# The order of VectorE's steps in the first attention phase of a four-layer kernel, and an early exponential on ScalarE

## The chip, the cores and the metric

The kernel runs on one core of a Trainium2 chip. The metric is the device time of one execution in microseconds (us). The median of three runs of the kernel before is 1622.35 us (1619.3 to 1623.19). The engines are TensorE (PE), VectorE (DVE), ScalarE (ACT), GpSimd (POOL) and SyncE (SP, which only issues transfers). Each has its own instruction stream; they meet at semaphores.

## The reference, cut to what matters

Sixteen tiles of 128 tokens with 256 values each go through four layers, each an attention and a feed-forward part. The change lies where layer 0's attention and layer 1's attention are computed:

```
x = x + L0_xattn(layernorm(x), ctx)   # softmax(q k^T + alibi, masked) v, 16 heads of 16, then out_w
x = x + L0_ffn(layernorm(x))          # shared expert, and eight routed experts (top 2)
x = x + L1_xattn(layernorm(x), ctx)   # per token: 16 heads against 16 heads, causal over heads
x = x + L1_ffn(layernorm(x))          # top 2 of eight experts
# layers 2 and 3 follow
```

Layer 0's attention is an ordinary one over 128 keys. Layer 1's is unusual: for each token alone, its 16 query heads attend to the 16 key heads of the same token's context row, so a tile's scores are 16x16 for each token. These are elementwise products and sums and run on DVE.

## The kernel before, in words

**Turns.** The sixteen tiles are four groups of four tiles (T = 4). A turn of `phase1` does layer 0 for one group: context columns, keys, values, query columns, attention, output projection, the residual add, and the shared expert. From the second turn on, the same turn does layer 1's attention for the group before, with its router's lists. So the first turn has none of that other layer's work, and turns 2, 3 and 4 have it. On PE and ACT turns 2 to 4 are one rolled loop; on DVE turns 2 and 3 are a loop, and turn 4 is written out. After turn 4 come the early expert tiles of layer 1, then the other layers.

**Layer 0's attention.** It goes by units: UNITS = 8 in a turn, two for each tile, eight heads in each. For unit n, PE writes a bias and the scores into two PSUM banks ("s"), DVE takes the negated row maxima (`maxima(n)`, line 1841, two reductions of 128x512), ACT takes exponentials (line 1464, eight of 128x128) and with them empties the banks, PE transposes the probabilities ("p", two banks, line 937), ACT copies them (line 1470), and PE multiplies them with the values ("v"). After both units of a tile ACT copies the sum (line 1457), PE transposes it back ("o", line 930), and DVE divides by the row sums (`norm_out(t)`: a reciprocal at line 1848, then a multiplication at line 1779 into `att_rows`). PE's order is `att_order`: at step n it does scores n, probabilities n-2, values n-3, and at odd n from 5 on the result of tile (n-5)/2.

**Banks.** Scores rotate over four banks, so scores n+2 want those of unit n emptied and so on. Probabilities and results rotate together over two banks, 4 and 5 (`PROB_RING`): p of units 0 to 3 take 4 and 5 in turn, tile 0's result takes 4, unit 4's first block takes 5 and its second block takes 4 again, after DVE has divided tile 0. In the same way unit 6's second block follows tile 1's result.

**Pieces.** The other layer's work on DVE is a list of pieces (`layer1_pieces`, `layer1_rows_out`): two for the normalization and the queries; for each of four tiles eight for the scores (four products m0 to m3 of growing width and four sums r0 to r3, in the order m0 m1 r0 m2 r1 m3 r2 r3); scale, largest and shift, with the mark "shifted"; total and inverse; eight for each of four tiles with the values; divide and add; and two for the next normalization, with the mark "end". That makes 75. `some(n)` does the next n of them, `until(mark)` does all up to the mark. Between "shifted" and total stands an exponential on ACT (`exps16`, line 1534). ACT does it in its own order at step `L1_SHIFT` of its loop, behind that unit's exponentials and copies.

**DVE's order in a turn, before.** 10 pieces; then for each unit n its maxima and 4 pieces; behind unit 5 the rest up to "shifted" (three more); behind unit 6's pieces the division of tile 0; then 4 pieces and the division of tile 1, 4 and tile 2, 4 and tile 3; then the remaining 18 pieces. Then it adds the projected rows ("xo") to the residual stream (after GpSimd's `x_biased`) and normalizes them for the feed-forward part.

**Tables.** ACT's exponential and its SiLU (in the feed-forward part) want different activation tables; copies and identities go with either. The loads are put into the program ahead of the activation that wants them.

Of the kernel before, what the change touches and what calls it, by code (L numbers as in the profile page):

```python
# [28 lines left out]
P = 128  # L29
TILES = 16  # L30
T = 4
# [116 lines left out]

L1_FRONT, L1_STEP, L1_SHIFT = 10, 4, 5


LATE = range(1, T)
# [9 lines left out]
def build(nc, ins, out):  # L164
# [7 lines left out]
    UNITS = 2 * T  # L172
# [119 lines left out]
    with ctx:  # L292
        def sb(name, shape, dt=F32):
            return ctx.enter_context(nc.sbuf_tensor(name, shape, dt))
# [55 lines left out]
        NA = sb("norm_rows_layer1", [P, T, D])  # L350
        PRDA = sb("products_dve", [P, 4 * H * HD])
        PAR = sb("head_parity", [P, 2])
        CKM = sb("k_bias_by_parity", [P, KC, 2])
        LGA = sb("router0_logits", [P, TILES * E])
        cT = sb("ctx_cols", [P, KC, T * P])
# [1070 lines left out]
        def _(act):  # L1426
# [6 lines left out]
            def copy_cols(plan, g, name, dst, bias=None):  # L1433

                for m in range(KC):
                    ps, b = full(plan, g, (name, m))
                    if bias is None:
                        act.activation(dst[:, m, :], ps[:, :], ACT.Copy).then_inc(bank_empty[b], 1)
                    else:
                        act.activation(dst[:, m, :], ps[:, :], ACT.Identity, bias=col_bias[:, bias, m:m + 1]).then_inc(bank_empty[b], 1)  # L1440

            def phase1(plan, turn, g, prev):
# [8 lines left out]
                    act.activation(V0[:, t, :, 0:HD], ps[:, 0:D].rearrange("p (h d) -> p h d", h=H), ACT.Copy).then_inc(bank_empty[b], 1)  # L1451
                copy_cols(plan, turn, "xT0", xT)
                copy_cols(plan, turn, "qT", qT, CQ0)
                for n in range(UNITS + 4):
                    if n >= 5 and n % 2 == 1:
                        ps, b = full(plan, turn, ("acc", "oT", (n - 5) // 2))
                        act.activation(OT[:, :], ps[:, :], ACT.Copy).then_inc(bank_empty[b], 1)
                    if n < UNITS:
                        u = n % SB
                        act.wait_ge(sem("maxima"), UNITS * g + (n + 1))  # L1460
                        for x in range(2):
                            ps, b = full(plan, turn, ("s", n, x))
                            for h in range(4 * x, 4 * x + 4):
                                last = act.activation(SC[:, u, h, :], ps[:, (h % 4) * P:(h % 4 + 1) * P], ACT.Exp, bias=MX[:, 32 + 8 * u + h:33 + 8 * u + h])  # L1464
                            last.then_inc(bank_empty[b], 1)
                    if 2 <= n < UNITS + 2:
                        i = n - 2
                        for x in range(2):
                            ps, b = full(plan, turn, ("p", i, x))
                            act.activation(PT[:, i % KB, 4 * x:4 * x + 4, :], ps[:, :].rearrange("p (h k) -> p h k", h=4), ACT.Copy).then_inc(bank_empty[b], 1)  # L1470
                    if n == L1_SHIFT and prev is not None:
                        exps16(prev + 1)
# [270 lines left out]
        def _(dve):  # L1743
# [87 lines left out]
            def phase1(plan, turn, g, prev, last_turn=False):  # L1831
# [4 lines left out]
                def maxima(i):  # L1836

                    for x in range(2):
                        ps, b = full(plan, turn, ("s", i, x))
                        at = 32 + 8 * (i % SB) + 4 * x  # L1840
                        last = dve.tensor_reduce(MX[:, at:at + 4], ps[:, :].rearrange("p (h k) -> p h k", h=4), AX, ALU.max, negate=True)  # L1841
                    last.then_inc(sem("maxima"), 1)

                def norm_out(t):
                    ps, b = full(plan, turn, ("o", t))
                    o = ps[:, :].rearrange("p (h d) -> p h d", h=H)
                    r = RC[:, H * (t % 2):H * (t % 2) + H]
                    d(dve.reciprocal(r, o[:, :, HD]))
                    settle()
                    tt(AO[:, t, :].rearrange("p (h d) -> p h d", h=H), o[:, :, 0:HD], bc(r, HD), ALU.mult).then_inc(bank_empty[b], 1)  # L1850

                some(L1_FRONT)
                for n in range(UNITS):
                    maxima(n)
                    some(L1_STEP)
                    if n == L1_SHIFT:
                        until("shifted")
                    if n >= 6 and n % 2 == 0:
                        norm_out((n - 6) // 2)
                some(L1_STEP)  # L1860
                norm_out(T - 3)
                some(L1_STEP)
                norm_out(T - 2)
                some(L1_STEP)
                norm_out(T - 1)
                until("end")
                dve.wait_ge(sem("x_biased"), g + 1)
                for t in range(T):
# [249 lines left out]
            class Pieces:  # L2118
# [4 lines left out]
                def some(self, count):  # L2123
                    for _ in range(count):
                        while self.left and isinstance(self.left[0], str):
                            self.left.pop(0)
                        if self.left:
                            self.left.pop(0)()

                def until(self, mark):  # L2130
                    while mark in self.left:
                        p = self.left.pop(0)
                        if not isinstance(p, str):
                            p()
# [976 lines left out]
```

## Time and profile before

| what | us |
|---|---|
| median of three runs | 1622.35 |
| the profiled execution's own time | 1619.95 |
| its span in the trace | 1618.2 |
| PE busy | 1325.2 (82%) |
| DVE busy | 830.0 (51%) |
| ACT busy | 448.3 (28%) |
| POOL busy | 286.4 (18%) |
| first maxima of turns 1 to 4 start at | 39.34, 129.74, 251.67, 376.72 |

Times in the rows are counted from the start of the span. An engine's shares are means over stages with different limits: the four turns of the first phase fill the first 460 us or so, and the layers after them the rest. An arrow in square brackets names what ended the idle time in front of an instruction, and how long the idle time was. PE's granted clock is 1.00 at the high and 0.50 at the low level.

### The profile page before, as it was taken

To read this page: it belongs to the slowest core of one execution; us is meant where nothing else is said; L and a number is where in the kernel's file an instruction comes from. 1 tells how busy PE (TensorE), PEld (TensorE's weight loads), DVE (VectorE), ACT (ScalarE), POOL (GpSimd) and SP (SyncE) were. 2 spreads that over 40 slices of the span, in tenths; PEclk is the share of its full clock that TensorE was granted. 3 is DMA by queue.
4 is the path that set the end of the run, shared out by engine and by line. 5 is a ranking of instruction groups with operands and counts; after the bars stand their busy time and mean duration, and the time that the engine had idled before them with its cause. 6 is when DMAs were issued, how large, how long until landed. Compare 5 with 4: busy or idle time off the path is not lost.

```text
span 1618.2 us, 25691 instructions
## 1 busy us (share of the span) xinstructions
PE 1325.2 (82%) x8174; PEld 1081.9 (67%) x8186; DVE 830.0 (51%) x2347; ACT 448.3 (28%) x1126; POOL 286.4 (18%) x307
## 2 busy tenths in 40 slices
PE   5877687677658897889977877868489999999997
PEld 3554454444447677888855656556379999999996
DVE  2249768768776767112244757575752222222222
ACT  2635225325322233111223332323121111111111
POOL 2010012012020002000124334441421111111111
PEclk9787677668668999999977988989799999999999
DMA  9996032023066277888501001010368888888984
GB/s 341 351 264 146 0 99 106 0 86 118 0 226 219 92 275 247 292 290 291 184 22 40 14 27 53 27 40 1 123 249 315 311 311 324 312 310 313 326 315 147
DMA packets 116318, 291.52 MB, mean 180 GB/s; under 512 B 8192, under 2 KB 90528, under 8 KB 101024
## 3 DMA queue, kind: packets, MB, share of 16 engines
q1 hardware_dynamic: 106032, 273.00, 48.4%
q0 software_dynamic: 10224, 17.77, 4.3%
q8 instruction: 30, 0.49, 0.1%
q14 instruction: 32, 0.26, 0.0%
HBM read 218.84 MB, written 71.90 MB: 180 GB/s over the span
## 4 chain that ended last, share of the span: by engine, by line
PE 51%; issue 19%; DVE 13%; POOL 6%; DMA 6%; ACT 3%; SPq 2%; DVEq 0%; POOLq 0%; ACTq 0%
PE bank L838 47%; DMA work<-in_moe 4%; POOL expert_rows_in L2898 3%; DVE work L2518 2%; DVE stats L1785 1%; ACT work L1464 1%; DVE row_max L1841 1%; PE bank L1140 1%; PE bank L937 1%; DVE x_stream L2518 1%; PE bank L1181 1%; DVE extra L2026 1%; POOL rstd L2863 1%; PE bank L845 1%; DVE extra L2029 1%
## 5 line engine op out<-in xcount | busy, mean ns | idle before, releaser
L838 PE MATMUL bank<-norm_cols,work 128*128 128x128 f32 x3488 | 435.2, 280 | 28.7 <-DMA work<-in_moe 17.2
L838 PEld LDWEIGHTS bank<-norm_cols,work 128*128 128x128 f32 x3488 | 424.8, 196 | 43.0 <-issue 24.9
L1779 DVE TENSOR_TENSOR extra<-bank,span 128x256 f32<-128x256 f32 x202 | 85.6, 425 | 386.9 <-ACT span L1563 386.9
L838 PE MATMUL bank<-work,extra 128*128 128x256 f32 x808 | 207.7, 381 | 0.0
L1563 ACT ACTIVATE span<-bank 128x256 f32<-128x256 f32 x202 | 77.4, 383 | 447.9 <-PE bank L838 447.9
L838 PEld LDWEIGHTS bank<-work,extra 128*128 128x128 f32 x808 | 139.0, 192 | 10.9
L3044 POOL DMA_INDIRECT out_x<-att_rows,slot_token x39 | 60.7, 1556 | 345.7 <-ACT att_rows L1573 304.8
L2863 POOL TENSOR_TENSOR rstd<-var_eps,neg_half 128x4 f32<-128x4 f32 x18 | 18.3, 1018 | 515.5 <-DVE var_eps L1791 515.5
L838 PE MATMUL bank<-norm_cols,weights 128*128 128x128 f32 (+2 forms) x416 | 90.8, 378 | 18.2 <-ACT norm_cols L1604 12.0
L838 PE MATMUL bank<-weights,norm_cols 128*128 128x512 f32 (+1 forms) x192 | 88.4, 609 | 8.3 <-ACT norm_cols L1604 5.5
L838 PEld LDWEIGHTS bank<-norm_cols,weights 128*128 128x128 f32 x416 | 68.0, 219 | 35.3 <-ACT norm_cols L1604 16.9
L838 PE MATMUL bank<-work 128*128 128x256 f32 (+4 forms) x260 | 63.9, 386 | 27.6 <-ACT work L1604 12.3
L1464 ACT ACTIVATE work<-bank,row_max 128x128 f32<-128x128 f32 x256 | 69.5, 389 | 44.5 <-DVE row_max L1841 44.4
L937 PE MATMUL bank<-ident,work 128*128 128x128 f32 x256 | 55.4, 378 | 29.3 <-DVE att_rows L1779 23.0
L1841 DVE TENSOR_REDUCE row_max<-bank 128x4 f32<-128x512 f32 x64 | 41.1, 684 | 66.9 <-PE bank L838 66.9
L937 PEld LDWEIGHTS bank<-ident,work 128*128 128x128 f32 x256 | 41.1, 192 | 47.1 <-DVE att_rows L1779 25.5
L838 PEld LDWEIGHTS bank<-work 128*128 128x128 f32 (+1 forms) x260 | 40.9, 203 | 45.0 <-ACT work L1604 11.7
L838 PEld LDWEIGHTS bank<-weights,norm_cols 128*128 128x128 f32 x192 | 40.3, 223 | 41.7 <-issue 27.8
L2870 POOL TENSOR_TENSOR rstd<-var_eps,neg_half 128x2 f32<-128x2 f32 x48 | 35.4, 738 | 174.0 <-DVE var_eps L1791 173.6
L838 PE MATMUL bank<-weights,ctx_cols 128*128 128x256 f32 x192 | 49.9, 416 | 0.0
L838 PE MATMUL bank<-work,q_cols 32*128 32x256 f32 x256 | 49.5, 518 | 0.0
L838 PEld LDWEIGHTS bank<-weights,ctx_cols 128*128 128x128 f32 x192 | 40.2, 214 | 7.9 <-issue 2.2
(361 smaller groups left out, 1978.6 us busy)
## 6 DMA issues: line engine op xcount, KB each, us to landing
work<-in_moe SPq DMA_DIRECT2D x39, 2048.0 KB, 8.1
work<-in_moe SPq DMA_DIRECT2D x70, 1024.0 KB, 9.4
expert_rows_in<-zero SPq DMA_DIRECT2D x3, 5590.0 KB, 52.3
expert_rows_in<-zero SPq DMA_DIRECT2D x3, 5504.0 KB, 36.0
expert_rows_out<-zero SPq DMA_DIRECT2D x3, 5504.0 KB, 22.4
work<-in_moe SPq DMA_DIRECT2D x31, 512.0 KB, 5.9
weights<-in_moe SPq DMA_DIRECT2D x8, 1024.0 KB, 5.6
att_cols<-expert_rows_in SPq DMA_DIRECT2D x39, 130.0 KB
```

The costliest lines, as they stand in the source:

```text
L838: return pe.matmul(o, l, r, start=a, stop=z)
L845: m = pe.transpose(ps[:, t * P:(t + 1) * P], rows[:, t, c * P:(c + 1) * P], ident[:, :])
L937: last = pe.transpose(ps[:, h * P:(h + 1) * P], SC[:, w, 4 * x + h, :], ident[:, :])
L1464: last = act.activation(SC[:, u, h, :], ps[:, (h % 4) * P:(h % 4 + 1) * P], ACT.Exp, bias=MX[:, 32 + 8 * u + h:33 + 8 * u + h])
L1563: act.activation(SG[:, b, :], ps[:, 0:256], ACT.Silu).then_inc(sem("silu_slots"), 1)
L1779: return dve.tensor_tensor(o, a, b, op)
L1841: last = dve.tensor_reduce(MX[:, at:at + 4], ps[:, :].rearrange("p (h k) -> p h k", h=4), AX, ALU.max, negate=True)
L2518: return dve.scalar_tensor_tensor(o, a, scalar, b, op0, op1)
L2863: pool.tensor_tensor(RS[:, :], VE[:, :], neg_half[:, :], ALU.pow).then_inc(sem("rstd" + stream), 1)
L2870: pool.tensor_tensor(RS[:, part], VE[:, part], neg_half[:, part], ALU.pow).then_inc(sem(f"rstd_s{u}"), 1)
L2898: pool.indirect_dma_start(out=rows_to, out_offset=bass.IndirectOffsetOnAxis(ap=IDXG[:, 2 * t + k:2 * t + k + 1], axis=0), in_=rows[:, t, : ...
L3044: pool.indirect_dma_start(out=out_rows, out_offset=bass.IndirectOffsetOnAxis(ap=SLOTI[:, u:u + 1], axis=0), in_=YS[:, u, :], in_offset=Non ...
```

## The change

Five edits. DVE does 14 pieces ahead of the first maxima instead of 10. The pieces behind the maxima of units 0 to 7 are 4, 3, 4, 3, 3, 3, 3 and 3 instead of 4 each, and the jump to "shifted" behind unit 5 is gone: all 32 score pieces are done behind unit 5, and scale, largest and shift are the three pieces behind unit 6. Tile 0 is divided ahead of unit 6's maxima; tile 1 directly behind unit 7's three pieces; then 4 pieces and tile 2, 4 pieces and tile 3, and 27 pieces remain. ACT takes `exps16` at step 6 instead of 5. And ACT computes one exponential of a 128x1 column behind the query columns, in all four turns; nothing reads its result.

```diff
-L1_FRONT, L1_STEP, L1_SHIFT = 10, 4, 5
+L1_FRONT, L1_STEPS, L1_TAIL, L1_SHIFT = 14, (4, 3, 4, 3, 3, 3, 3, 3), (4, 4), 6
...
+        EXPW = sb("exp_ready", [P, 1])
...
                 copy_cols(plan, turn, "qT", qT, CQ0)
+                act.activation(EXPW[:, :], PAR[:, 0:1], ACT.Exp)
...
                 some(L1_FRONT)
                 for n in range(UNITS):
+                    if n == UNITS - 2:
+                        norm_out(0)
                     maxima(n)
-                    some(L1_STEP)
-                    if n == L1_SHIFT:
-                        until("shifted")
-                    if n >= 6 and n % 2 == 0:
-                        norm_out((n - 6) // 2)
-                some(L1_STEP)
-                norm_out(T - 3)
-                some(L1_STEP)
-                norm_out(T - 2)
-                some(L1_STEP)
-                norm_out(T - 1)
+                    some(L1_STEPS[n])
+                norm_out(1)
+                for t in range(2, T):
+                    some(L1_TAIL[t - 2])
+                    norm_out(t)
                 until("end")
```

## Rows read from the trace of the kernel before

**Rows 1.** Windows: attention of turns 1 to 4, and a stretch of turn 3.
```profile
core 0: us, PE busy (x) PEld busy (x) DVE busy (x) ACT busy (x) POOL busy (x), PEclk, DMA share, GB/s
39.00:87.00 48.00, 37.85 (x295) 24.28 (x294) 13.14 (x25) 28.52 (x86) 0.00 (x0) 0.79 1.06 342
129.00:191.00 62.00, 43.00 (x293) 27.31 (x292) 52.02 (x76) 31.42 (x88) 0.00 (x0) 0.64 0.27 62
251.00:314.00 63.00, 42.58 (x290) 26.67 (x290) 51.97 (x75) 31.46 (x88) 2.65 (x2) 0.67 0.05 16
376.00:437.00 61.00, 41.76 (x292) 26.26 (x290) 51.26 (x75) 31.39 (x88) 0.00 (x0) 0.69 0.01 4
...
280.00:296.00 16.00, 11.08 (x67) 6.71 (x66) 10.63 (x16) 6.37 (x18) 0.00 (x0) 0.50 0.00 0
```

**Rows 2.** Timeline of DVE in turn 3: start, duration, instruction, idle time before.
```profile
251.67 1.29 DVE L1841 TENSOR_REDUCE row_max<-bank 128x4 f32<-128x512 f32 x2 [4.27 <-PE bank L838]
252.88 1.08 DVE L1779 TENSOR_TENSOR products_dve<-span,ctx_rows_layer 128x256 f32<-128x256 f32 x1
...
270.29 1.29 DVE L1841 TENSOR_REDUCE row_max<-bank 128x4 f32<-128x512 f32 x2 [0.87 <-PE bank L838]
...
293.14 1.29 DVE L1841 TENSOR_REDUCE row_max<-bank 128x4 f32<-128x512 f32 x2 [5.20 <-PE bank L838]
...
307.14 0.26 DVE L1848 RECIPROCAL row_rec<-bank 128x16 f32<-128x16 f32 x1 [2.82 <-PE bank L930]
```

**Rows 3.** Timeline of DVE, turn 3: one score tile (m1, r2 left out).
```profile
262.04 0.42 DVE L1779 TENSOR_TENSOR products_dve<-span,ctx_rows_layer 128x256 f32<-128x256 f32 x1
...
262.97 0.41 DVE L2026 TENSOR_REDUCE extra<-products_dve 128x16 f32<-128x256 f32 x1
263.42 0.96 DVE L1779 TENSOR_TENSOR products_dve<-span,ctx_rows_layer 128x768 f32<-128x768 f32 x1
264.30 1.28 DVE L1841 TENSOR_REDUCE row_max<-bank 128x4 f32<-128x512 f32 x2
265.49 0.68 DVE L2026 TENSOR_REDUCE extra<-span 128x32 f32<-128x512 f32 x1
266.20 1.22 DVE L1779 TENSOR_TENSOR span<-span,ctx_rows_layer 128x1024 f32<-128x1024 f32 x1
...
268.21 1.21 DVE L2026 TENSOR_REDUCE extra<-span 128x64 f32<-128x1024 f32 x1
```

**Rows 4.** Timeline of PE in turn 3.
```profile
257.61 2.08 PE L838 MATMUL bank<-work,q_cols 32*128 32x256 f32 x8
...
273.44 1.13 PE L838 MATMUL bank<-work,q_cols 32*128 32x256 f32 x8
...
287.99 1.12 PE L937 MATMUL bank<-ident,work 128*128 128x128 f32 x4 [4.92 <-DVE att_rows L1779]
...
301.20 1.12 PE L937 MATMUL bank<-ident,work 128*128 128x128 f32 x4 [2.81 <-DVE att_rows L1779]
```

**Rows 5.** Timeline of ACT in turn 3, at the first exponentials.
```profile
253.06 1.28 ACT L1464 ACT_TABLE_LOAD   x1 [3.21 <-DVE row_max L1841]
254.35 2.17 ACT L1464 ACTIVATE work<-bank,row_max 128x128 f32<-128x128 f32 x8
```

**Rows 6.** Timeline of DVE, turns 2 and 4: first maxima and third division.
```profile
129.74 1.29 DVE L1841 TENSOR_REDUCE row_max<-bank 128x4 f32<-128x512 f32 x2 [0.29 <-PE bank L838]
...
183.78 0.26 DVE L1848 RECIPROCAL row_rec<-bank 128x16 f32<-128x16 f32 x1 [3.03 <-PE bank L930]
...
376.72 1.29 DVE L1841 TENSOR_REDUCE row_max<-bank 128x4 f32<-128x512 f32 x2 [6.40 <-PE bank L838]
...
430.10 0.26 DVE L1848 RECIPROCAL row_rec<-bank 128x16 f32<-128x16 f32 x1 [2.75 <-PE bank L930]
```

**Rows 7.** Timeline of turn 1: unit 4's second block, and the third division.
```profile
65.66 1.12 PE L937 MATMUL bank<-ident,work 128*128 128x128 f32 x4 [0.95 <-DVE att_rows L1779]
...
80.86 0.26 DVE L1848 RECIPROCAL row_rec<-bank 128x16 f32<-128x16 f32 x1 [4.08 <-PE bank L930]
```

## The prediction, on record before the changed kernel ran

> **What bounds the kernel now.** I read the share of engines by stretch first, then VectorE's (DVE's) instructions in time, then what TensorE (PE) and ScalarE (ACT) waited for. In the attention stretch of the first turn, which carries no pieces of the other layer, DVE works 13 of 48 us; in the three later turns it works 51 to 52 of 61 to 63 us [rows 1]. From there to the end of the turn (through the last piece, the output normalization and the residual add) it hardly stops, and the next PE work waits for it. So the end of a later turn is the work of DVE plus its idle time. The work is not changed by the edit: the same 75 pieces, 8 maxima and 4 divisions are issued, in another order. What can change is the idle time, and that is four gaps in the third turn [rows 2]: 4.27 us before the first maxima, two short ones (0.87 and another of 0.77 us), 5.20 us before the eighth maxima, 2.82 us before the third division. The fourth turn has 6.40 us in place of 4.27; the second only 0.29 [rows 6], since its DVE came late.
>
> The 5.20 us are made by DVE itself. Unit 4's second block of transposed probabilities wants the PSUM bank that holds tile 0's result. It starts at 287.99, after a wait of 4.92 us for `att_rows` [rows 4], that is for the division of tile 0, which stands behind the seventh maxima and four pieces. The eighth maxima's scores are behind it on PE. The 2.82 us before the third division have the same kind of cause: unit 6's second block waits 2.81 us for the second division [rows 4].
>
> **The price of a step.** Taking start to start in one tile of eight pieces [rows 3]: the first two products 0.93, first sum 0.45, third product 0.88, (a maxima pair 1.19), second sum 0.71, fourth product and third sum 2.01, last sum 1.11. A tile is 6.1 us. A division is 0.70 (0.25 and 0.42 with a gap).
>
> **Front 10 to 14 pieces.** The four added are 0.93 + 0.45 + 0.88 = 2.26 us. In turns 3 and 4 they fit into the 4.27 and 6.40 us before the first maxima, so that wait becomes 2.0 and 4.1 us. In turn 2 there is no room (0.29): the first maxima go from 129.74 to 131.7.
>
> **The table.** ACT_TABLE_LOAD takes 1.28 us at 253.06, after the first maxima, and the first exponential starts at 254.35, 0.01 us behind it [rows 5]. The small exponential behind the query columns draws it forward, into a gap of ACT of 3.2 us (the load's own row gives it). So the first exponentials of a turn come 1.29 us after where they could be; the edit gives 1.29 to that chain in three turns, and costs at most one short ACTIVATE in that gap, which I take as nothing. If the gap were not there it would cost 0.2 to 0.4 us, as the other small ones do (an exponential of 128x128 is 0.27 of the 2.17 us that eight take). The first turn has no load there.
> The Trainium skill, "ScalarE: Activation LUTs", section What ACT_TABLE_LOAD costs, says a switch is 1283 ns for the load and about 1380 ns of drain. The load agrees with the 1.28 here; of a drain behind it the 0.01 us leave nothing. By the page the table part would be worth 2.66 us per turn instead of 1.29.
>
> **Third turn walked through, PE at the speeds it had.** The second part of a unit's scores takes PE 2.08 us at the low clock and 1.13 at the high one [rows 4]; with the bias part ahead of it that is some 3.0 and 1.7. By the same ratio a unit's transposes are 2.0 or 1.1 (1.12 for four at the low level [rows 4]), its values 1.1 or 0.7. Maxima 0 at 251.67 as before, then four pieces (3.83), maxima 1 at 256.7; three pieces (1.38), maxima 2 at 259.3 (before, 1.2 ahead of 262.04 [rows 3], so 260.8); four (3.60), maxima 3 at 264.1. Exponentials 2 are then 1.5 us earlier than before, and what hangs on them too: scores 4 are full at 269.0, but three pieces (2.04) leave DVE free at 267.4: 1.6 idle. Maxima 5 wait for scores 5 until 273.6, 1.4 idle. Tile 0's result on PE wants the probabilities of unit 3 copied, 278.4; DVE divides at once (0.4 idle), and unit 4's second block follows the first without the 4.92 us wait. Maxima 6 at 281.0 (1.9 idle), then scale, largest, shift (3.66), maxima 7 at 287.1 (1.2 idle), 6.0 us earlier than 293.14. With three pieces behind them DVE is free at 290.3, but tile 1's result waits for ACT's copy of unit 5: 292.2, 1.8 idle. From the end of that division to the third division the chain on PE took 6.0 us (301.20 to 307.14, and 0.06 ahead of it), so 298.9; four pieces are 2.65: 3.4 idle. Then 3.5 us of pieces and the fourth division.
>
> So the idle time is not gone, it has moved: 13.9 us before, about 13.7 after. By position: the third division comes at 298.9 instead of 307.14, but with 9 pieces fewer done by then, 7.2 us (2.01 + 1.11 + 0.93 + 0.45 + 0.88 + 0.71 + 1.15). That equals 306.1, **1.0 us gained** (0.2 of it idle time, most of the rest a product that took 1.08 us at 252.88 while GpSimd worked [rows 2], and that now lies in the idle time in front). In the fourth turn the same 47.2 us from the first maxima plus 7.2 stand against 53.4 (430.10 - 376.72) [rows 6]: 1.0 lost, of which its earlier high clock gives about 1.0 back: **0**. In the second turn 131.7 + 47.2 + 7.2 = 186.1 against 183.78: 2.3 lost, 0.8 given back by the same reason: **1.5 lost**. In the first turn unit 4's second block loses its 0.95 us wait for the division [rows 7]: **0.95 gained**. Sum with the PE speeds of before: 0.5 us gained, which is nothing. Bounds of this sum: if DVE idled nowhere from the first maxima on (less 2.0, 0 and 4.1 in front), 11 us per turn more, 33; if it idled as in the walk and each walk error of 0.5 us at eight waits had one sign, 4 us per turn the other way, 12.
>
> **The clock.** PE's granted clock is 0.64 to 0.69 in these stretches [rows 1], half the time at the low level (1.2 GHz). From 280 to 296 it is 0.50 throughout: it fell after PE had waited for unit 3's copies, stayed low over the 4.92 us wait, rose at the end of the unbroken work from 287.99, and fell again in the 2.81 us wait. With the change PE works unbroken from 278.4 to about 290, and before the third division's chain only waits of about 1 us are left. I take it that the clock is high in that chain: then it takes the 4.1 us of the first turn (its DVE waits 4.08 us from one division to the next [rows 7]) in place of 6.0 [rows 4], and DVE's 3.4 idle becomes 1.5: 1.9 us per turn, 5.7 in three. The lower end is 0 (low clock, as in the rows), the upper that of the second rival.
> The Trainium skill, "TensorE: Matmul & The Clock Gate", section What's actually happening, says that the moment of the rise varies between runs of one kernel. If so, this term differs from run to run and the forecast loses in sharpness; by that rule the sum would be anywhere from 0.5 to 6.2 us. The trace agrees so far that the second, third and fourth turn, one code, had 0.64, 0.67 and 0.69.
>
> **Sum.** 0.5 + 5.7 = 6.2 us. The profiled execution took 1619.95 us (span 1618.2 and 1.75 around it), 2.4 below the median of the runs, so 1613.8 of its kind and **1616.1** against the median 1622.35. What follows the fourth turn (scatter, gathered rows, early experts) hangs on it in one chain, so I pass the gain on whole. Weights and lists are loaded by other queues long before; no DMA is moved.
>
> **Rivals.**
> (a) The idle time only moves. All walks as above, clock as before: 0.5 us, 1621.9. For it: 9 pieces (7.2 us) go behind the last division in each turn, and steps of three pieces (2.0) are shorter than PE's 3 + 2 + 1.1 us per unit at the low clock. Against: two waits that kept PE idle (4.92 and 2.81) go. Also here: the small exponential doesn't take the load with it (1.29 lost in three turns, 1620 instead of 1616).
> (b) The clock is high from scores 6 on. Scores 6 and 7 save 0.9 and 1.3, DVE then never waits for maxima 7, the result of tile 1 comes at 289.7 and the third division at 294.4 rather than 298.9: 4.5 more per turn than the walk, 13.5 + 0.5 = 14 us, 1608. For it: PE's longest break is gone. Against: its work from 287.99 to 296 was unbroken as well and low nearly to its end.
> (c) Slower. The mechanism is the shorter steps: DVE's work is put off by 7.2 us per turn, and the turn is longer from the point at which the third division comes less than 7.2 us earlier than before. If the stretch that was high (scores 5 at 1.13 us for the second part [rows 4], then transposes, values, result) turns low, as the fuller PE of the walk's start meets another phase of the clock, that is 1.3 + 0.9 + 0.4 = 2.6 us per turn and the third division at 301.5, 1.6 us too late per turn; with both the second turn's loss and no gain from the clock: 7.8 - 0.5 = 7.3 us, 1629.6. For it: the second turn has no front room. Against: in the fourth turn the high level held over two waits of that size.
>
> **Chances.** Forecast 0.40 (its own range 3 to 9 us gained, 1613 to 1619), (a) 0.23, (b) 0.19, (c) 0.18. A difference below 0.3% (4.9 us) can't be told from none. Of the forecast two thirds are above 4.9: faster 0.27 + 0.19 = 0.46, same 0.13 + 0.23 = 0.36, slower 0.18. Range 1608 to 1627: it leaves out half of (b)'s and half of (c)'s chance, 0.19.
>
> **What would show it.** In the changed profile: no load before the first exponential, which starts 1.4 us after the maxima's start; first maxima still at 251.67 minus what the turns before gave, and 2 us later than its neighbours in the second turn; no wait of PE for `att_rows` before unit 4's second block; DVE idle before the fifth and sixth maxima (1.6 and 1.4), before the second division (1.8) and the third (1.5 if the clock is high, 3.4 if low); granted clock over 0.70 in the three stretches. Wrong would be: DVE waits of over 3 us before the third division in all turns, or total idle from first maxima to third division unlike 9 to 14 us.

## The result, and the profile after

The changed kernel takes 1614.39 us in the median of 14 runs (1606.89 to 1619.53) against 1622.95 for the kernel before in runs beside it (1617.25 to 1627.22). The ratio is 0.9951, 95% interval 0.9938 to 0.9963: 8 us, half a per cent, faster. The forecast was 1616.1. Its profiled execution has a span of 1612.4 us (before 1618.2). In a later set of runs the same program came out at 0.9981 (0.9966 to 0.9995) of the kernel before, so the gain is 3 to 8 us, and a ratio from one set of runs is good to some 0.3%.

Windows of the changed kernel, the same columns as [rows 1]; the four attention stretches:

```profile
39.00:87.00 48.00, 37.30 (x304) 24.19 (x305) 13.61 (x26) 28.85 (x86) 0.00 (x0) 0.86 1.06 343
129.00:191.00 62.00, 44.88 (x310) 28.68 (x306) 54.61 (x80) 30.35 (x89) 0.00 (x0) 0.75 0.21 53
249.00:312.00 63.00, 46.85 (x306) 30.09 (x302) 52.24 (x75) 30.04 (x87) 2.66 (x2) 0.72 0.04 15
370.00:433.00 63.00, 45.86 (x310) 29.59 (x308) 53.16 (x77) 30.63 (x89) 0.37 (x1) 0.74 0.02 9
```

PE's granted clock is higher in all four: 0.86 for 0.79 in the first, 0.72 to 0.75 for 0.64 to 0.69 in the others. In the trace of the later set it is 0.71 to 0.74 in those three.

DVE's timeline in turn 3, which answers to [rows 2]. The line numbers have moved by two:

```profile
249.27 1.29 DVE L1843 TENSOR_REDUCE row_max<-bank 128x4 f32<-128x512 f32 x2 [2.06 <-issue]
254.69 1.27 DVE L1843 TENSOR_REDUCE row_max<-bank 128x4 f32<-128x512 f32 x2
257.14 1.27 DVE L1843 TENSOR_REDUCE row_max<-bank 128x4 f32<-128x512 f32 x2
261.92 1.28 DVE L1843 TENSOR_REDUCE row_max<-bank 128x4 f32<-128x512 f32 x2
267.35 1.29 DVE L1843 TENSOR_REDUCE row_max<-bank 128x4 f32<-128x512 f32 x2 [2.09 <-PE bank L839]
271.83 1.29 DVE L1843 TENSOR_REDUCE row_max<-bank 128x4 f32<-128x512 f32 x2 [1.28 <-PE bank L839]
276.65 0.26 DVE L1850 RECIPROCAL row_rec<-bank 128x16 f32<-128x16 f32 x1 [0.41 <-PE bank L931]
279.14 1.29 DVE L1843 TENSOR_REDUCE row_max<-bank 128x4 f32<-128x512 f32 x2 [1.78 <-PE bank L839]
284.45 1.29 DVE L1843 TENSOR_REDUCE row_max<-bank 128x4 f32<-128x512 f32 x2 [0.37 <-PE bank L839]
289.27 0.26 DVE L1850 RECIPROCAL row_rec<-bank 128x16 f32<-128x16 f32 x1 [1.54 <-PE bank L931]
295.01 0.26 DVE L1850 RECIPROCAL row_rec<-bank 128x16 f32<-128x16 f32 x1 [2.51 <-PE bank L931]
```

The walk had said idle times of 2.0, 1.6, 1.4, 0.4, 1.9, 1.2, 1.8 and 3.4 us at these places. They are 2.06, 2.09, 1.28, 0.41, 1.78, 0.37, 1.54 and 2.51. Five waits of 13.9 us together have become eight of 12.0 us, none over 2.6. Four more pieces lie ahead of the first of them.

What stood behind the 5.20 and 2.82 us is gone. In PE's timeline of the same turn only one wait for `att_rows` is left inside the attention, where [rows 4] had 4.92 and 2.81 us:

```profile
277.04 2.08 PE L839 MATMUL bank<-work,q_cols 32*128 32x256 f32 x8
...
282.94 1.48 PE L839 MATMUL bank<-work,q_cols 32*128 32x256 f32 x8
...
290.04 0.71 PE L938 MATMUL bank<-ident,work 128*128 128x128 f32 x4 [0.32 <-DVE att_rows L1781]
```

The first two rows are also clock readings. This part of scores 6 takes 2.08 us, as at the low level. The same part of scores 7 takes 1.48 us, between 2.08 and the 1.13 of the high level: the clock rose while it ran. PE's waits for ACT's copies of probabilities remain: 2.55 us ahead of tile 0's result (2.53 before) and 2.55 us ahead of tile 1's (1.22 before).

ACT's timeline there, which answers to [rows 5]. The load and the small exponential lie directly behind the query columns, ahead of a gap:

```profile
247.45 1.28 ACT L1455 ACT_TABLE_LOAD   x1
248.75 0.20 ACT L1455 ACTIVATE exp_ready<-head_parity 128x1 f32<-128x1 f32 x1
250.67 2.18 ACT L1466 ACTIVATE work<-bank,row_max 128x128 f32<-128x128 f32 x8 [1.72 <-DVE row_max L1843]
```

**A ledger.** GpSimd computes one power for each normalization, and the starts of these rows cut the turns cleanly: from the power ahead of the other layer's queries to the power behind the last piece. Turn 3 of the changed kernel, from 236.21 to 322.72, is 86.51 us:

```profile
236.21 1.01 POOL L2861 TENSOR_TENSOR rstd<-var_eps,neg_half 128x4 f32<-128x4 f32 x1 [3.53 <-DVE var_eps L1793]
...
322.72 1.04 POOL L2861 TENSOR_TENSOR rstd<-var_eps,neg_half 128x4 f32<-128x4 f32 x1 [71.04 <-DVE var_eps L1793]
```

The same stretch for turns 2, 3 and 4, and DVE's idle time in it from its timeline (the bracketed times ahead of maxima and divisions), in every kernel of the study:

| kernel | turns 2, 3, 4 | sum | DVE idle | sum less idle | median, ratio to before |
|---|---|---|---|---|---|
| before | 85.49, 88.90, 89.11 | 263.5 | 38.0 | 225.6 | 1622.95, 1 |
| changed | 83.16, 86.51, 86.37 | 256.0 | 31.0 | 225.1 | 1614.39, 0.9951 |
| changed, again | 84.55, 85.68, 86.37 | 256.6 | 31.7 | 224.9 | 1613.97, 0.9981 |
| early division only | 81.57, 82.50, 85.23 | 249.3 | 23.6 | 225.7 | 1608.42, 0.9929 |
| early exponential only | 86.43, 86.69, 91.40 | 264.5 | 38.5 | 226.0 | 1622.04, 1.0036 |
| changed, no early exponential | 84.92, 86.09, 85.98 | 257.0 | 32.3 | 224.7 | 1611.27, 0.9945 |
| changed, division behind | 87.67, 90.37, 91.95 | 270.0 | 45.6 | 224.4 | 1629.94, 1.0079 |
| changed, 10 in front | 85.05, 86.51, 87.15 | 258.7 | 34.0 | 224.7 | 1618.65, 1.0009 |
| changed, steps of 4 | 82.13, 84.61, 85.84 | 252.6 | 27.8 | 224.8 | 1606.58, 0.9936 |
| changed, waits filled | 80.48, 82.43, 83.07 | 246.0 | 21.7 | 224.3 | 1603.72, 0.9891 |
| changed, fillers on PE | 81.13, 81.88, 83.09 | 246.1 | 19.6 | 226.5 | 1601.14, 0.9880 |
| longer steps | 79.43, 79.44, 82.64 | 241.5 | 15.7 | 225.8 | 1598.65, 0.9885 |
| longer steps and fillers | 78.01, 77.39, 80.37 | 235.8 | 11.1 | 224.6 | 1587.88, 0.9818 |

The medians come from four sets of runs, in which the kernel before took 1622.95, 1619.97, 1616.74 and 1617.25 us; so rows are compared by their ratios and not by their medians.

The column that counts is the last but one: in all thirteen traces it is 224.3 to 226.5. The stretch is DVE's work, which no order changes much, plus the time DVE waits in it. That alone says nothing of causes. It says where to look, and the experiments then show which edit moved which wait.

The highest value, 226.5, has a cause that the trace shows. In turn 3 of that kernel a DVE product of 128x1024, 1.22 us elsewhere, ran beside a GpSimd addition and took 3.39 us:

```profile
241.14 2.35 POOL L2879 TENSOR_TENSOR x_stream<-x_stream,row_bias 128x1024 f32 x1
...
241.20 3.39 DVE L1785 TENSOR_TENSOR span<-span,ctx_rows_layer 128x1024 f32<-128x1024 f32 x1
```

In the changed kernel's turn 3 the same addition was nearly over when that product began (249.33 and 2.35, against 251.18), and the product took 1.59 us. So DVE's work does depend a little, by up to 2.2 us in a turn, on what GpSimd does beside it.

What the first phase gained doesn't reach the end unchanged. In the changed kernel the last of these powers comes 8.16 us earlier (442.35 against 450.51), the span is 5.8 shorter. The stretch behind it lies between 1165.9 and 1176.6 us in the thirteen traces (before 1167.7, changed 1170.1), with no relation to the edits that can be seen; so a single span is worth less than the ledger, and the medians more. The first turn varies as well. From its first power to its last it took 68.1 to 72.4 us in the eleven traces without fillers on PE, and 69.82 and 68.13 us in two traces of the changed kernel.

### The profile page after: what moved, and what is told of

Its sections match the earlier page's. It is cut to its first block, busy times and chain, and to the rows that moved or that the text cites. A ratio compares the mean times of both kernels' runs of the same rounds, so it can differ in the third digit from the quotient of the medians.

```text
span 1612.4 us, 25699 instructions
## 1 busy us (share of the span) xinstructions
PE 1319.4 (82%) x8186; PEld 1076.2 (67%) x8186; DVE 829.6 (51%) x2347; ACT 449.9 (28%) x1130; POOL 287.8 (18%) x307
## 4 chain that ended last, share of the span: by engine, by line
PE 50%; issue 19%; DVE 12%; POOL 7%; DMA 6%; ACT 3%; SPq 2%; another core or an unknown queue 0%; DVEq 0%; POOLq 0%; ACTq 0%
PE bank L839 46%; DMA work<-in_moe 3%; POOL expert_rows_in L2896 3%; DVE work L2516 2%; DVE stats L1787 1%; ACT work L1466 1%; PE bank L938 1%; POOL rstd L2861 1%; PE bank L1141 1%; PE bank L1182 1%; DVE x_stream L2516 1%; POOL work L2939 1%; ACT norm_cols L1606 1%; DVE extra L2027 1%; DVE row_max L1843 1%
## 5 line engine op out<-in xcount | busy, mean ns | idle before, releaser
L839 PEld LDWEIGHTS bank<-work,extra 128*128 128x128 f32 x808 | 138.8, 191 | 10.8
L839 PEld LDWEIGHTS bank<-work 128*128 128x128 f32 (+1 forms) x260 | 41.9, 208 | 45.2 <-POOL head_of_row L3014 11.5
L938 PE MATMUL bank<-ident,work 128*128 128x128 f32 x256 | 51.4, 362 | 4.4 <-ACT work L1472 3.0
L846 PE MATMUL bank<-ident,norm_rows_layer 128*128 128x128 f32 x32 | 7.2, 390 | 53.1 <-DVE norm_rows_layer L1799 53.1
```

Source lines behind the costliest of these rows:

```text
L839: return pe.matmul(o, l, r, start=a, stop=z)
L938: last = pe.transpose(ps[:, h * P:(h + 1) * P], SC[:, w, 4 * x + h, :], ident[:, :])
```

## The experiments

All ratios are to the kernel before, run beside. The theory tested (A): a later turn ends when DVE has done its work and its idle time, and the gain is what the edits take from that idle time. The other question (B) was what PE's clock adds.

### The early division alone

```diff
                 for n in range(UNITS):
+                    if n == UNITS - 2:
+                        norm_out(0)
                     maxima(n)
                     some(L1_STEP)
                     if n == L1_SHIFT:
                         until("shifted")
-                    if n >= 6 and n % 2 == 0:
-                        norm_out((n - 6) // 2)
```

> The kernel before with one edit: tile 0 is divided ahead of unit 6's maxima instead of behind its four pieces. Steps, front, shift and table stay. Theory A (the end of a turn is DVE's work plus its idle time, and the 5.20 us idle are made by the late division): unit 4's second block follows the first; in turn 3 the division lies at 283.4, the eighth maxima's scores are full near 289.4 and DVE is free at 287.9, so 1.4 us idle instead of 5.2; the 2.8 us before the third division stay. Gain 3.8 us in three turns and 1 in the first: 10 to 12 us, 0.993 to 0.994. Rival (the idle time only moves behind: the second division then waits for ACT's copies, as in the changed kernel): 3 to 5 us, 0.997 to 0.998, with 1 to 2 us idle before the second division. If the gain of the changed kernel comes from the shorter steps, this one shows none.

Measured: 0.9929 (0.9906 to 0.9952), 1608.42 us. One move of one division gives 11.5 us. By the stretches that is clearly more than the whole change (14.2 us against 6.9 to 7.5), while the intervals of the two ratios overlap (0.9906 to 0.9952, and 0.9938 to 0.9963). Its timeline of DVE in turn 3, and PE's wait there:

```profile
276.60 0.25 DVE L1848 RECIPROCAL row_rec<-bank 128x16 f32<-128x16 f32 x1
...
277.22 1.28 DVE L1841 TENSOR_REDUCE row_max<-bank 128x4 f32<-128x512 f32 x2
281.56 1.29 DVE L1841 TENSOR_REDUCE row_max<-bank 128x4 f32<-128x512 f32 x2 [0.47 <-PE bank L838]
288.86 0.25 DVE L1848 RECIPROCAL row_rec<-bank 128x16 f32<-128x16 f32 x1
295.08 0.26 DVE L1848 RECIPROCAL row_rec<-bank 128x16 f32<-128x16 f32 x1 [2.34 <-PE bank L930]
```

```profile
277.36 1.11 PE L937 MATMUL bank<-ident,work 128*128 128x128 f32 x4 [1.83 <-DVE att_rows L1779]
```

The 5.20 us before the eighth maxima are 0.47, the wait before the third division stays (2.34), and no new one has come before the second. Over the three turns the wait before the eighth maxima falls from 5.20 each to 0.55, 0.47 and 1.43 us, 13.2 of the 14.2 us of the stretches. The rival fell.

### The early division taken out of the change

```diff
                 for n in range(UNITS):
-                    if n == UNITS - 2:
-                        norm_out(0)
                     maxima(n)
                     some(L1_STEPS[n])
+                    if n == UNITS - 2:
+                        norm_out(0)
```

> The changed kernel with tile 0's division put back behind unit 6's maxima and their three pieces (scale, largest, shift); all else stays. Theory A: unit 4's second block waits on PE until that division, the eighth maxima come some 4.5 us later in each of turns 2 to 4 (idle before them about 5 us instead of 0.4 to 1), less the 0.4 to 0.7 us DVE now waits ahead of the division: 11 to 14 us slower than the changed kernel, so 3 to 6 us slower than the kernel before, 1.002 to 1.004. Rival (short steps and the fuller front bring a part of the gain by themselves): 0.996 to 0.999.

Measured: 1.0079 (1.0057 to 1.0102), 1629.94 us: slower than before by 13 us, more than expected. The stretches sum to 270.0, 14.0 more than the changed kernel's; alone the division had given 14.2 (263.5 to 249.3). In turn 3 the eighth maxima wait as they did before, and PE for the division:

```profile
291.91 1.29 DVE L1843 TENSOR_REDUCE row_max<-bank 128x4 f32<-128x512 f32 x2 [5.20 <-PE bank L839]
```

```profile
286.77 1.12 PE L938 MATMUL bank<-ident,work 128*128 128x128 f32 x4 [4.60 <-DVE att_rows L1781]
```

So the division is the whole gain, and the rest of the change without it costs 6.5 us of the stretches (270.0 against 263.5).

### The early exponential: taken out, and alone

```diff
-                act.activation(EXPW[:, :], PAR[:, 0:1], ACT.Exp)
```

> The changed kernel without the small exponential behind the query columns. Theory A: the load of 1.28 us is back before the first exponentials of turns 2 to 4, the chain of exponentials and scores is 1.3 us later, and DVE idles that much more before the fifth maxima (2.09 becomes 3.4 in turn 3): 3 to 4 us of the 8 are lost, against the kernel before 0.997 to 0.998. Rival (the load is hidden anyway, since DVE has work up to the fifth maxima): 0.995 as with it.

Measured: 0.9945 (0.9928 to 0.9963), against 0.9951 with it; stretches 257.0 against 256.0 and 256.6. The load is back at its place, 1.28 us long, and it makes little difference. DVE waits 0.46 to 0.47 us before the third maxima in each of the three turns, 1.4 us together, that it had not with the early exponential. In turn 3 it waits 0 instead of 2.09 us before the fifth, but that is PE's clock: the second part of those scores took 1.13 us here and 2.08 in the changed kernel's trace. Here theory A's expectation was wrong and the rival right.

The same line put into the kernel before, alone:

> The kernel before with the small exponential behind the query columns and nothing else. Theory A: the chain of exponentials is 1.3 us earlier, but DVE waits little for it (0.8 us before the fourth or fifth and sixth maxima), so at most 0.3 to 0.9 us in each of turns 2 to 4: 1 to 2 us in all, 0.999 to 1.000; the 5.20 and 2.8 us waits, which DVE makes itself, stay. Rival (the load is on the way of every turn's end, as the prediction took it): 4 us, 0.9975.

Measured: 1.0036 (1.0018 to 1.0054), 1622.04 us, stretches 264.5 against 263.5. Not a gain in any case. Whether it is a loss stays open: its trace explains 1 us of 5. The waits of 5.20 us stayed, as expected, and those before the third division are 3.00, 1.75 and 3.03 us. The first turn, which runs the small exponential too, took 72.43 us against 71.07, within what it varies by.

### Ten pieces in front

```diff
-L1_FRONT, L1_STEPS, L1_TAIL, L1_SHIFT = 14, (4, 3, 4, 3, 3, 3, 3, 3), (4, 4), 6
+L1_FRONT, L1_STEPS, L1_TAIL, L1_SHIFT = 10, (8, 3, 4, 3, 3, 3, 3, 3), (4, 4), 6
```

> The changed kernel with 10 pieces in front of the first maxima and 8 behind them, instead of 14 and 4; all else stays. Theory A: turns 3 and 4 idle 2.3 us more before the first maxima, and give nothing back, since DVE reaches the second maxima that much later: 4 to 5 us slower than the changed kernel, 0.997 to 0.998 of the kernel before; turn 2 the same within 0.5 us. Rival (the earlier first maxima start the chain of exponentials and scores earlier, and idle behind the fifth maxima shrinks by as much): 0.995.

Measured: 1.0009 (0.9992 to 1.0026), stretches 258.7, 2.1 to 2.7 more than the changed kernel's. The wait before the first maxima is 5.49 and 5.99 us in turns 3 and 4 (2.06 and 3.78 with 14), but most of that comes back behind: DVE waits 0.97 and 1.22 us instead of 1.78 and 1.61 before the seventh maxima, 0 instead of 0.37 and 0.97 before the eighth, 2.10 and 1.70 instead of 2.51 and 2.55 before the third division. In turn 3 the fifth and sixth maxima also wait less, 1.50 and 0 us instead of 2.09 and 1.28. Turn 3 is as long as in the changed kernel (86.51), turn 4 0.8 us longer. By its stretches the rival is nearer to the truth; by its ratio the edit costs 5 to 9 us, which the trace doesn't explain. The changed kernel run again (below) shows differences of that size for one program, so the worth of the front stays open between 2 us and more.

### Steps of four

```diff
-L1_FRONT, L1_STEPS, L1_TAIL, L1_SHIFT = 14, (4, 3, 4, 3, 3, 3, 3, 3), (4, 4), 6
+L1_FRONT, L1_STEPS, L1_TAIL, L1_SHIFT = 14, (4, 4, 4, 4, 4, 3, 4, 4), (4, 4), 5
```

> The changed kernel with steps of four: 14 in front, then 4, 4, 4, 4, 4, 3, 4, 4 behind the maxima and 4, 4 between the last divisions, the other layer's exponential at step 5; early division and table stay. It has all of the change but the single steps (and the shift is done at the same place by count as before). Theory A (the shorter steps make DVE wait for PE and cost what the division gained): 3 to 7 us better than the changed kernel, attention stretches of turns 2 to 4 249 us or less together as with the early division alone (249.3; changed kernel 256.0, before 263.5), 0.990 to 0.993. Rival (the four pieces less before the shift let DVE wait 1.5 us before unit 6's maxima, and the order is no better than the changed one): 0.995.

Measured: 0.9936 (0.9912 to 0.9960), beside it the changed kernel 0.9981; stretches 252.6, 3.4 to 4.0 better than the changed kernel's and 3.3 worse than with the early division alone. So the steps of three cost about 4 us of stretch, together with the later place of the shift and of `exps16`, which this run moves back as well; the two weren't tested apart. The fuller front with steps of four isn't free either: its four pieces are missing behind the sixth maxima, and DVE waits 1.81 and 1.37 us before the last two maxima in turn 3 (0 and 0.47 with the division alone).

### The changed kernel once more

> The changed kernel once more, beside the two others, since times of one kernel differ by some us between runs and the run with 10 pieces in front came out 5 us worse than its trace explains. Both theories: 0.994 to 0.9965. Its trace: attention stretches of turns 2 to 4 together 254 to 259 us, and the stretch behind the first phase anywhere from 1166 to 1177 us as in the traces so far. A sum outside 254 to 259 would say that the order of DVE doesn't fix the time of these stretches.

Measured: 0.9981 (0.9966 to 0.9995), 1613.97 against 1617.25 us; stretches 256.6. The ledger repeats within 0.6 us, the ratio doesn't: 0.9951 and 0.9981 lie further apart than their intervals.

### The waits filled with pieces

```diff
-L1_FRONT, L1_STEPS, L1_TAIL, L1_SHIFT = 14, (4, 3, 4, 3, 3, 3, 3, 3), (4, 4), 6
+L1_FRONT, L1_STEPS, L1_TAIL, L1_SHIFT = 14, (4, 3, 4, 3, 3, 3, 3, 5), (5, 4), 6
```

> The changed kernel with 5 pieces instead of 3 behind unit 7's maxima and 5 instead of 4 between the second and third division: three pieces more, put where DVE waits (1.54 us before the second division, 1.02 to 2.55 before the third). Theory A: 1.05 us of pieces fit into the first wait and about 2 us into the second, idle before the two divisions falls from 4.05 to under 1 us in turns 3 and 4 and from 2.56 to 0.5 in turn 2: 7 to 9 us better than the changed kernel, 0.989 to 0.991 of the kernel before. Rival (what the waits gave has to be paid behind: PE gets the second and third tile's banks later and the last division is late, or the tail of the turn has its own wait): 0.994 to 0.996.

Measured: 0.9891 (0.9869 to 0.9913), 1603.72 us. The waits before the second and third division are 0.60 and 0.32 us in turn 3, and the stretches 246.0: three pieces in the right place give 10 us, a little over what was expected.

### Fillers on PE

```diff
                     elif a == "o":
+                        if i < 2:
+                            spare = fill(plan, turn, ("s", 6, 0) if i == 0 else ("acc", "oT", 2))[0]
+                            for _ in range(8):
+                                mm(spare[:, :], identb[:, :], SBIAS[:, 0, :, :, :].rearrange("p c a k -> p (c a k)"))
                         ready(plan, turn, ("acc", "oT", i))
```

> The changed kernel with 8 extra bias products (128x512, bf16) on PE in each of its two longest waits of a turn, ahead of the results of tiles 0 and 1, into banks that are free then; their results are overwritten. It keeps PE at work over the 2.55 us waits. Theory B (the clock's level decides the rest): the granted clock stays at 1.00 behind these waits, scores 6 and 7 take 1.7 instead of 2.6 to 3.0 us, the way from second to third division 4.1 instead of 5.0, and DVE's idle falls by 2 to 2.5 us in turns 3 and 4, less in turn 2, which was high already: 4 to 7 us better than the changed kernel, 0.991 to 0.993 of the kernel before. Rival (the level doesn't follow such work, or DVE's order decides): 0.995, or some tenths of a us per turn worse where the fillers delay a result.

The second bank already holds unit 4's half of tile 2's sum at that point, so this kernel computes tile 2's attention from the wrong products; the order and the shapes of the other instructions are the same. Measured: 0.9880 (0.9857 to 0.9902), 1601.14 us. It is a gain of 10 us in the stretches, more than expected, and of 2 to 4 in the first turn (65.97 us against 68.13 and 69.82). PE in turn 3, with the fillers in the first row and the same parts of scores 6 and 7 behind them, which took 2.08 and 1.48 us in the changed kernel:

```profile
264.09 1.90 PE L839 MATMUL bank<-work,ident_bf 128*128 128x512 bf16 x8
...
266.98 1.13 PE L839 MATMUL bank<-work,q_cols 32*128 32x256 f32 x8
...
270.19 1.13 PE L839 MATMUL bank<-work,q_cols 32*128 32x256 f32 x8
```

Windows of turn 3 around the two fillers, first in this kernel, then in the changed one:

```profile
268.00:281.00 13.00, 10.30 (x108) 6.55 (x110) 11.02 (x16) 9.88 (x26) 0.00 (x0) 1.00 0.00 0
```

```profile
276.00:289.00 13.00, 10.45 (x76) 6.68 (x76) 9.03 (x13) 8.24 (x23) 0.00 (x0) 0.74 0.00 0
```

PE is busy as long in both; with the fillers it does 108 instructions in that time instead of 76 (the fillers among them), all at the high level. The third division's wait is 1.02 us in all three turns (2.51 and 2.55 without in turns 3 and 4).

### Longer steps, without and with fillers

```diff
-L1_FRONT, L1_STEPS, L1_TAIL, L1_SHIFT = 14, (4, 3, 4, 3, 3, 3, 3, 3), (4, 4), 6
+L1_FRONT, L1_STEPS, L1_TAIL, L1_SHIFT = 14, (4, 4, 4, 4, 3, 4, 6, 6), (6, 4), 5
```

> The changed kernel with longer steps: 14 in front, then 4, 4, 4, 4, 3, 4, 6, 6 pieces behind the eight maxima, 6 and 4 between the last divisions, the exponential of the other layer at step 5 again, tile 0's division ahead of unit 6's maxima. Theory A (idle time of DVE is all that an order can give): idle from first maxima to third division falls from 10.0, 8.3 and 6.8 us to 2 to 3 (some 1.5 of it before unit 6's maxima): 15 to 20 us better than the changed kernel, 0.982 to 0.986 of the kernel before. Rival (from some point PE's results come too late and the last transposes and products of a turn end it): 0.989 like the fuller tail alone.

Measured: 0.9885 (0.9862 to 0.9909), 1598.65 us. The stretches are 241.5, 14.5 less than the changed kernel's, just under the 15 to 20 expected. Idle from first maxima to third division is 3.1, 2.6 and 4.1 us. The gain by the ratio, 18 us, is smaller than expected (0.982 to 0.986); the first turn took 72.07 us from its first power to its last here, 69.82 and 68.13 in the changed kernel's two traces, and has no pieces that the edit could touch.

The fillers again, the second one ahead of unit 4's values, whose first product overwrites it:

```diff
+                def filler(ps):
+                    for _ in range(8):
+                        mm(ps[:, :], identb[:, :], SBIAS[:, 0, :, :, :].rearrange("p c a k -> p (c a k)"))
...
                     elif a == "o":
+                        if i == 0:
+                            filler(fill(plan, turn, ("s", 6, 0))[0])
...
                             ps_o, b_o = fill(plan, turn, ("acc", "oT", t))
+                            if i == 4:
+                                filler(ps_o)
```

> The longer steps of the run before, and 8 extra bias products on PE ahead of tile 0's result and ahead of unit 4's values, each into a bank that is overwritten afterwards, so that the result is the full one. Theory B (clock) says that where DVE no longer waits for PE, a higher clock gives little in turns 2 to 4: 0 to 4 us better than the longer steps alone, most of it in the first turn (4 us with the fillers before) and before unit 6's maxima. Rival: the fillers' gain of 13 us over the changed kernel adds in full, 0.974 to 0.978.

Measured: 0.9818 (0.9798 to 0.9838), 1587.88 us, the best of the study and 29 us better than the kernel before. Over the longer steps alone it is 10.8 us in the medians and 10.7 in the spans: 6.4 us come in the first turn, which has no pieces, and 5.7 in the stretches, while the stretch behind the first phase is 2.7 longer. Part of the 6.4 can be the spread of that turn: without fillers it took 68.1 to 72.4 us, and 65.7 here. Neither expectation (0 to 4, and 13 or more) was met. DVE in turn 3, from the fifth maxima on:

```profile
256.98 1.29 DVE L1851 TENSOR_REDUCE row_max<-bank 128x4 f32<-128x512 f32 x2 [0.96 <-PE bank L839]
260.90 1.28 DVE L1851 TENSOR_REDUCE row_max<-bank 128x4 f32<-128x512 f32 x2
266.99 0.25 DVE L1858 RECIPROCAL row_rec<-bank 128x16 f32<-128x16 f32 x1
267.62 1.28 DVE L1851 TENSOR_REDUCE row_max<-bank 128x4 f32<-128x512 f32 x2
272.72 1.28 DVE L1851 TENSOR_REDUCE row_max<-bank 128x4 f32<-128x512 f32 x2
278.70 0.25 DVE L1858 RECIPROCAL row_rec<-bank 128x16 f32<-128x16 f32 x1
284.48 0.25 DVE L1858 RECIPROCAL row_rec<-bank 128x16 f32<-128x16 f32 x1
```

One wait of 0.96 us is left there, and one of 2.12 before the first maxima.

## Why the prediction was right, and where only its sum was

**What bounds a turn: right.** That the end of a later turn is DVE's work plus its idle time was the base of the walk. Thirteen traces hold it to 2.3 us in 225, and the one that is highest has a product that GpSimd's addition made 2.2 us longer. (The prediction counts four gaps in turn 3; the ones that it names are five, 13.9 us.)

**The division: right, and under-weighed.** The prediction saw that unit 4's second block waits for tile 0's division behind the maxima and four pieces, and its wait did go. But the walk booked it together with the steps of three, at 0.5 us net, and didn't ask what that part would bring with the steps left alone: 14.2 us of stretch and 11.5 in the medians, shown by adding it alone and by taking it out.

**The steps of three: right in kind.** The walk put 1.6, 1.4, 1.9, 1.2 and 1.8 us of new idle time behind them and called the result of turns 2 to 4 about nothing. Measured it is a loss of 3.4 to 4.0 us of stretch against steps of four (with the earlier shift), and 6.5 for all of the change but the division. Rival (c) named the mechanism and was wrong on the size, as the division outweighs it.

**The front: mostly right.** Filled waits of 4.27 and 6.40 us became 2.06 and 3.78 (2.0 and 4.1 said), and in turn 2 the first maxima came at 131.67 (131.7 said). In the kernel run again these are 3.10, 3.83 and 130.19. But by the stretches it is worth 2.1 to 2.7 us and not the 4.5 of the two filled waits, since most comes back behind.

**The early exponential: wrong.** The walk let the 1.29 us count fully, and its expectations with it. Exponentials 0 do start 1.4 us after the maxima's start, but taken out or put in alone the edit moves the stretches by some 1 us or less, where the changed kernel differs from itself by 0.6. With pieces in hand, DVE waits little for exponentials 0: no idle stands before the second to fourth maxima, and without the edit 0.46 to 0.47 us stand before the third.
The Trainium skill, "ScalarE: Activation LUTs", section What ACT_TABLE_LOAD costs, gives a further 1380 ns of drain for a switch. In the changed kernel the small exponential starts 0.02 us behind the load (248.75 against 247.45 and 1.28), and the load starts within 0.01 us of the end of the activation ahead of it (246.75 and 0.69), so no drain is seen on either side of it.

**The walk by turns.** It said 0.95, -1.5, 1.0 and 0 us, and 1.9 for the clock in each of turns 2 to 4: 0.4, 2.9, 1.9. Measured in the stretches: 2.3, 2.4, 2.7 (0.9, 3.2 and 2.7 in the kernel run again), and 1.3 in the first turn (71.07 to 69.82 from its first power to its last), which is less than that turn varies by in one kernel. Turn 2 was the furthest off: there the clock rose to 0.75 from 0.64. Total idle from first maxima to third division was to be 9 to 14 us by the prediction's own test. It was 6.8, 10.0 and 8.3 us in turns 2, 3 and 4, so two of three turns fell outside.

**The clock term: right in direction, half in size.** From the second division's end to the third division it was to be 4.1 us instead of 6.0. It is 3.55 in turn 2 (169.65 + 0.70 to 173.90), but 5.04 and 5.09 in turns 3 and 4 (and 5.06, 5.04 and 5.11 in the kernel run again). That gives 4.3 of the 5.7 us in the one trace and 2.8 in the other. The clock did rise in the unbroken work before. It fell again at about 290.7, some 2 us behind the end of a wait of 2.55 us for ACT's copies of unit 5, which the prediction had put at about 1 us. The fillers show the rest: with PE kept at work there the level stays at 1.00. Two of the prediction's readings of the clock were off too. A mean of 0.64 to 0.69 between levels of 0.50 and 1.00 is 62 to 72% of the time at the low one, not half. And in the fourth turn before the change the high level held over waits of 0.22 and 0.59 us and fell just behind one of 1.70 us, which is weaker support against rival (c) than it says.
The Trainium skill, "TensorE: Matmul & The Clock Gate", section What's actually happening, lets the moment of the rise vary between runs of one kernel. That agrees: turn 2 of the changed kernel took 83.16 us in one trace and 84.55 in another, with the idle time accounting for the difference.

So the forecast of 6.2 us hit 8 (and 3 in the later runs) partly by luck. Of its 6.2 us, 5.7 were for the clock and 0.5 for the order. In the three stretches the clock gave at most 4.3 or 2.8 of the 7.5 or 6.9 us measured, which leaves 3 to 4 us for the order, where the walk had 0.5 lost. Two errors offset each other: too much for the table and the clock, too little for the division.

## What to carry to other kernels

Where one engine's idle time ends a stage, keep a ledger: stage length less that engine's idle time must be a constant over all orders (as long as no other engine slows that one's instructions), and each edit is then judged by the waits it removes and those it makes. Look first for a result that holds a shared buffer and stands behind other work of the same engine (here one division of 0.7 us, 14 us in three turns). Test the parts of a bundle alone: here one part gave all and the others took half of it back.

## What the runs showed of the hardware that was not expected

Sixteen idle bias products per turn on PE, of no use to the result, made the kernel some 11 us faster (0.9951 to 0.9880, and side by side 0.9885 to 0.9818), by keeping the granted clock at the high level over PE's waits in the middle of a turn: part of scores 6 and 7 went from 2.08 and 1.48 us to 1.13 each in turn 3. A GpSimd addition of 2.35 us made a DVE product that ran beside it take 3.39 us instead of 1.22, and 1.08 instead of 0.42 in the kernel before. One program's ratio to its neighbour differed by 0.3% between two sets of runs (0.9951 and 0.9981), more than either interval, while the sum of its attention stretches agreed within 0.6 us in 256 (single turns by up to 1.4). And the stretch behind the first phase, the same code in all kernels, took between 1165.9 and 1176.6 us in thirteen single traces.
